# Multi-query attention sandwich: which steps' row sums go to TensorE, where the turned maxima land, and how wo is loaded

## The chip, the cores and the metric

One NeuronCore of one Trainium2 chip runs the whole program. The metric is device microseconds of one execution. An instruction sits on one of five engines: PE (TensorE), DVE (VectorE), ACT (ScalarE), POOL (GpSimd) and SP (SyncE, which here only issues DMAs).

## The reference, cut to what matters

`x` is 2 x 2048 tokens of 1024 numbers, in float32. There are 32 query heads of 32 numbers, and a single head of keys and values that all of them share.

```
def attn(x, wq, wk, wv, wo):
    q = (x @ wq).reshape(B, T, 32, 32); k = x @ wk; v = x @ wv
    scores = einsum('bqhd,bkd->bhqk', q, k) / sqrt(32), causal
    probs = softmax(scores)
    return einsum('bhqk,bkd->bqhd', probs, v).reshape(B, T, C) @ wo
x = x + layernorm(attn(layernorm(x), wq, wk, wv, wo))
x = x + layernorm(ffn(layernorm(x)))      # 8 routed low-rank experts, softmax router
```

The softmax needs, for each query and head, the maximum of its scores and the sum of the exponentials over all keys. The change touches who forms that sum.

## The kernel before, in words

**Units.** Tokens are cut into 8 blocks of 512 (4 for each of the two sequences). A block has 8 units n of 4 heads, so there are 64 units. `qb_of(n)` is the block's place in its sequence, 0 to 3. Block b has the units 8b to 8b+7, and u = n % 8. A unit goes through its keys in steps of 128 keys: `steps(n)` is 4, 8, 12 or 16. The last four steps of a unit lie on the causal diagonal, and their tiles are 512, 384, 256 and 128 queries wide. Each step has 4 slots, one for each head g; slot j is step j // 4, head j % 4. The units of blocks 3 and 7 (units 24 to 31 and 56 to 63) have 16 steps, 64 slots.

**A step.** For each slot PE forms the transposed scores of one head into one of two PSUM banks (`scores`, L1299 to L1312), and ACT takes the exponential into the SBUF ring `pr`, which holds NS = 3 steps (`exps`, L707 to L715). PE multiplies the finished step with the values (`values`, L1314 to L1327) in the next step, at g = 1, or at g = 2 for a diagonal step, whose triangle POOL first sets to zero (`mask`, L621 to L627). The sum over keys is split: for most steps POOL adds the four heads' tile into `ds` (`add`, L604 to L619). For the steps that `by_pe` names, PE multiplies the tile with a column block of ones instead and accumulates in PSUM bank PAUX (L1328 to L1336). `sum_keys` (L1352 to L1359) then adds ds's column sums in the same bank, in slot 6 of the next unit, and DVE takes reciprocals there and scales the result (L953 to L961).

**Who waits for the sums.** ACT may write step k of the ring only when step k - 3 was used by both its readers: `exps` waits for `pv_done` of step k - 3, and, if POOL sums that step, for `added`. POOL runs in the order of its loop (L647 to L663): at step t first mask(t), which waits for all four exponentials of step t, and then add(t - 1). The first add of a unit takes steps 0 and 1 together (L616), all later ones are L619.

**Maxima.** For coming units PE also forms the scores in the other orientation (`max_scores`, L1286 to L1297) into a ring of NPM = 3 PSUM banks, and DVE takes their maxima (L931 to L940). When a unit's maxima are complete, PE turns them into rows (`max_rows`, L1339 to L1350) in PAUX, ACT copies them to `mT` (L705), and four DMAs of SP (L517) put them below the stacked queries. That must be there before the unit's first scores.

**Order of the rest.** Everything else is spread over the slots of the units by `pieces` (L113 to L163): projections of queries ("q"), of keys and values ("kv"), of the output ("proj"), the router and experts, the norms of the next block. Each engine goes through its own slots in order, so a piece that waits holds up all that stands behind it on that engine. Bank PX is shared by these pieces: `BEFORE` (L446 to L465) lists who had it last, and `bank_left` waits until that one was copied out. `value_turn` (L1385 to L1392) turns the next block's values once in u = 5, in PAUX. SP's list has the loads: `wo` in one DMA of 4 MB in unit 3, "ffn" in unit 1.

## Time and profile before

| | |
|---|---|
| median of 3 runs | 3544.06 us (3539.41 to 3547.18) |
| the profiled execution | 3543.98 us, its span 3542.2 us |
| mean granted TensorE clock | 0.968 |
| PE busy | 3302.0 us, 93% of the span |
| DVE busy | 2292.4 us, 65% |
| POOL busy | 2121.0 us, 60% |
| ACT busy | 1570.5 us, 44% |

A row of the timeline gives start, duration, engine, line, operation, out<-in, how many instructions it merges, and in brackets how long the engine stood idle before it and what ended that. A row of the chain gives start, length and the line that the end of the program goes back to at that moment. A float32 product is shown as two matmul records, so x8 in a row of L1326 or L1335 is one step's four heads.

### The profile page before, as it was taken

How to read it: one execution, taken by the hardware profiler on the slowest of the kernel's cores; microseconds unless marked ns; L12 is line 12 of the kernel's file. 1: busy time of each engine (PE TensorE's matmuls, PEld its weight loads, DVE VectorE, ACT ScalarE, POOL GpSimd, SP SyncE). 2: the span in 40 equal slices, each digit the busy share in tenths (PEclk: the TensorE clock that was granted, in tenths of full speed). 3: DMA queues.
4: the chain of work that ended last, by engine and by line, in shares of the span. 5: the costliest groups of instructions: out<-in, count | busy, mean ns of one | idle time of the engine just before them, and what ended most of it. 6: DMA issues, size and time to landing. Idle time of an engine off the chain costs nothing.

```text
span 3542.2 us, 45007 instructions
## 1 busy us (share of the span) xinstructions
PE 3302.0 (93%) x15784; PEld 1611.6 (45%) x15784; DVE 2292.4 (65%) x5974; ACT 1570.5 (44%) x3124; POOL 2121.0 (60%) x773
## 2 busy tenths in 40 slices
PE   7889999999999999999888999999999999999997
PEld 3444444444544444443444444444445444444433
DVE  4666766677767677773455667766677676666605
ACT  2324444444545444455322244444445454445552
POOL 1325676666666777767322266666666677766870
PEclk9989999999999999999998899999999999999998
DMA  4412111111101010010111121111011010001000
GB/s 117 114 46 67 48 43 37 53 29 40 37 22 54 22 34 28 22 37 16 61 54 43 46 67 45 36 37 61 27 36 35 25 28 28 28 28 28 27 1 24
DMA packets 132898, 144.01 MB, mean 41 GB/s; under 512 B 28088, under 2 KB 93624, under 8 KB 132672
## 3 DMA queue, kind: packets, MB, share of 16 engines
q1 hardware_dynamic: 132368, 140.72, 13.6%
q8 instruction: 125, 2.05, 0.2%
q14 instruction: 101, 0.83, 0.1%
q10 hardware_dynamic: 304, 0.41, 0.0%
HBM read 72.91 MB, written 16.78 MB: 25 GB/s over the span
## 4 chain that ended last, share of the span: by engine, by line
PE 58%; POOL 21%; DVE 10%; issue 5%; ACT 4%; SPq 1%; DMA 1%; POOLq 0%; ACTq 0%; DVEq 0%
POOL ds L619 15%; PE ps L1308 10%; PE ps L1326 10%; PE ps L1420 9%; PE ps L1296 8%; PE ps L1282 8%; DVE mx L940 4%; POOL ds L616 3%; ACT pr L715 2%; PE ps L1335 2%; PE ps L1357 2%; PE ps L1449 2%; POOL xr L636 1%; PE ps L1461 1%; PE ps L1381 1%
## 5 line engine op out<-in xcount | busy, mean ns | idle before, releaser
L715 ACT ACTIVATE pr<-ps 128x512 f32<-128x512 f32 (+3 forms) x2560 | 1304.7, 533 | 1533.3 <-PE ps L1308 1044.8
L619 POOL TENSOR_TENSOR ds<-ds,pr 128x2048 f32<-128x2048 f32 (+1 forms) x376 | 1518.6, 4039 | 189.3 <-ACT pr L715 161.2
L1308 PE MATMUL ps<-qs,ks 98*128 98x512 f32 (+3 forms) x2560 | 1368.5, 540 | 79.8 <-ACT pr L715 66.5
L940 DVE TENSOR_REDUCE mx<-ps 128x1 f32<-128x512 f32 x1536 | 996.9, 682 | 432.1 <-PE ps L1296 427.0
L1296 PE MATMUL ps<-ks,qs 96*128 96x512 f32 (+3 forms) x2560 | 970.7, 389 | 34.5 <-DVE mx L940 19.1
L1308 PEld LDWEIGHTS ps<-qs,ks 98*128 98x128 f32 x2560 | 492.3, 193 | 767.8 <-ACT pr L715 486.2
L937 DVE CUSTOM_DVE_ANT_0 ps<-ps,mask_qk 128x128 f32<-128x128 f32 (+3 forms) x1024 | 491.8, 497 | 438.4 <-PE ps L1296 434.5
L1326 PE MATMUL ps<-pr,vs 128*32 128x512 f32 (+3 forms) x5120 | 616.3, 554 | 6.9 <-POOL pr L626 6.8
L1296 PEld LDWEIGHTS ps<-ks,qs 96*128 96x128 f32 x2560 | 497.9, 196 | 269.6 <-issue 138.6
L1282 PE MATMUL ps<-xT,wq_sb 128*128 128x512 f32 x1024 | 525.4, 613 | 14.0 <-DVE ks L1001 9.7
L616 POOL TENSOR_TENSOR ds<-pr 128x2048 f32<-128x2048 f32 (+1 forms) x64 | 273.8, 4278 | 354.8 <-ACT pr L715 354.8
L1420 PE MATMUL ps<-wo_sb,ao 128*128 128x512 f32 x896 | 459.6, 610 | 24.3 <-DVE q L929 24.3
L626 POOL TENSOR_SCALAR_AFFINE_SELECT pr<-pr 128x512 f32<-128x512 f32 x192 | 123.2, 642 | 365.4 <-ACT pr L715 365.0
L956 DVE RECIPROCAL ps<-ps 128x128 f32<-128x128 f32 x256 | 244.3, 956 | 109.8 <-PE ps L1357 109.6
L1282 PEld LDWEIGHTS ps<-xT,wq_sb 128*128 128x128 f32 x1024 | 184.4, 192 | 177.8 <-issue 158.5
L1420 PEld LDWEIGHTS ps<-wo_sb,ao 128*128 128x128 f32 x896 | 160.6, 192 | 158.9 <-issue 119.4
L1326 PEld LDWEIGHTS ps<-pr,vs 128*32 128x32 f32 x5120 | 102.0, 109 | 194.1 <-issue 160.0
L645 POOL TENSOR_TENSOR xr<-xr,zs 128x1024 f32<-128x1024 f32 x28 | 66.1, 2361 | 201.7 <-ACT zs L769 201.7
L937 DVE DVE_READ_ACCUMULATOR2_ANT mx<- 128x1 f32 x1024 | 145.4, 142 | 0.0
L929 DVE TENSOR_TENSOR q<-ps,q 128x512 fp32r<-128x512 f32 x64 | 44.3, 692 | 124.8 <-ACT q L699 124.6
L615 POOL COPY ds<-pr 128x512 f32<-128x512 f32 x16 | 9.8, 609 | 157.2 <-ACT pr L715 157.2
L1335 PE MATMUL ps<-pr,ones 128*32 128x512 f32 (+3 forms) x1088 | 102.9, 451 | 0.0
(161 smaller groups left out, 1962.5 us busy)
## 6 DMA issues: line engine op xcount, KB each, us to landing
qs<-q SPq DMA_DIRECT2D x762, 64.0 KB, 2.0
wq_sb<-in_L_attn_wq_dram SPq DMA_DIRECT2D x64, 512.0 KB, 4.3
t<-in_L_attn_x_dram SPq DMA_DIRECT2D x32, 512.0 KB, 6.4
xr<-in_L_attn_x_dram SPq DMA_DIRECT2D x28, 512.0 KB, 3.6
out_dram<-xr SPq DMA_DIRECT2D x28, 512.0 KB, 2.6
wo_sb<-in_L_attn_wo_dram SPq DMA_DIRECT2D x1, 4096.0 KB, 14.5
qs<-mT SPq DMA_DIRECT2D x252, 4.0 KB
xT<-in_L_attn_x_dram SPq DMA_DIRECT2D x4, 512.0 KB, 5.3
```

What stands on the lines that cost most here:

```text
L616: nc.gpsimd.tensor_tensor(ds[:, :, c0:], first[:, :, c0:], this, ALU.add).then_inc(added, 1)
L619: nc.gpsimd.tensor_tensor(ds[:, :, c0:], ds[:, :, c0:], this, ALU.add).then_inc(added, 1)
L715: nc.scalar.activation(pr[:, k % NS, g, c0:], ps[:, PST + head(n, t, g) % NPS, c0:], ACT.Exp, scale=SCALE).then_inc(exp_done, 1)
L937: nc.vector.tensor_tensor_reduce(out=seen, in0=seen, in1=mask_qk[:, BLK - w:], op0=ALU.add, op1=ALU.max, scale=1.0, scalar=3.0 * NEG, accu ...
L940: nc.vector.tensor_reduce(found, seen, AX.X, ALU.max).then_inc(mx_done, 1)
L956: nc.vector.reciprocal(part, part).then_inc(rden_ready, 1)
L1282: last = nc.tensor.matmul(ps[:, PX, :], wq_sb[:, n % NW, k, :], xT[:, k, :], start=(k == 0), stop=(k == KT - 1))
L1296: nc.tensor.matmul(ps[:, bank, 0:w], qs[0:STK, n % NS, g, qt * P:(qt + 1) * P], ks[0:STK, c:c + w], start=True, stop=True).then_inc(mx_rea ...
L1308: last = nc.tensor.matmul(ps[:, bank, c0:], ks[0:STK + 2, c:c + P], qs[0:STK + 2, n % NS, g, c0:], start=True, stop=not by_mask)
L1326: last = nc.tensor.matmul(ps[g * HD:(g + 1) * HD, PPV, c0:], vs[:, row, :], pr[:, (UNIT_STEP[n] + t) % NS, g, c0:], start=(t == 0), stop=( ...
L1335: last = nc.tensor.matmul(ps[g * HD:(g + 1) * HD, PAUX, c0:], ones[:, :], pr[:, (UNIT_STEP[n] + t) % NS, g, c0:], start=(t == first), stop ...
L1420: last = nc.tensor.matmul(ps[:, PX, :], ao[:, (n + k) % NAO, j % TB * P:(j % TB + 1) * P], wo_sb[:, k, h * HALF:(h + 1) * HALF], start=(k ...
```

## The change

It has five parts.

1. `by_pe(n)` now gives a tuple of steps. In units of `qb_of` 2 it is (8, 9, 10, 11), as before. In units of `qb_of` 3 it is (5, 8, 11, 14, 15) for all u, where it was steps 12 to 15 for u = 0 to 5 and steps 10 to 15 for u = 6 and 7. POOL adds the others, so steps 12 and 13 too. `adds_in` counts POOL's adds; every wait on `added` uses it.
2. The turned maxima go to the ring of the maxima: the list `RING` has all users of the three banks in PE's order, and `max_bank_left` waits for the one three places earlier, be it a maximum (DVE) or rows (ACT's copy). PAUX is so free from the reciprocals on; the first PE sum of a unit waits for `ao_ready` of the unit before.
3. `value_turn` uses bank PX and its order of users ("vt" is in `BEFORE`); it stands in slot 10 (16-slot units) or N // 2, where it stood in slot 11 or N // 2 + 1, behind the "q" pieces of that slot.
4. `wo` is loaded in eight DMAs of 512 KB, two in each of units 2 to 5; the first "proj" waits for all of them.
5. "ffn" goes from slot 8 to slot 0 of unit 1 in SP's list.

```diff
     def by_pe(n):
-        if qb_of(n) < 2:
-            return 0
-        return TB + 2 if qb_of(n) == 3 and n % NU >= 6 else TB
+        return ((), (), (8, 9, 10, 11), (5, 8, 11, 14, 15))[qb_of(n)]
+
+    def adds_in(n, t):
+        return sum(x not in by_pe(n) for x in range(1, max(t, 1) + 1))
...
-        UNIT_ADD.append(UNIT_ADD[-1] + steps(n_) - 1 - by_pe(n_))
+        UNIT_ADD.append(UNIT_ADD[-1] + adds_in(n_, steps(n_) - 1))
...
+    def rows_slot(n):
+        return slots(n - 1) // 2 + max(4, slots(n - 1) // 8)
+
+    RING, PLACE, ROWS_PLACE = [], [], []
+    for k_ in range(HEADS + 1):
+        while len(ROWS_PLACE) < UN and (goal(len(ROWS_PLACE) - 1, rows_slot(len(ROWS_PLACE))) if ROWS_PLACE else FIRST_GOAL) <= k_:
+            ROWS_PLACE.append(len(RING))
+            RING.append(("rows", len(ROWS_PLACE) - 1))
+        if k_ < HEADS:
+            PLACE.append(len(RING))
+            RING.append(("max", k_))
...
+        if n and u == 5 and blk < LAST:
+            turned = 10 if N == 16 else N // 2
+            put(turned, "PE", "vt", blk + 1)
+            put(turned, "DVE", "vt", blk + 1)
...
-            at(64 + 32, "SP", "ffn")
-            at(64 * 3 + 32, "SP", "wo")
+            at(64 + 2, "SP", "ffn")
+            for k in range(KT):
+                at(64 * (2 + k // 2) + 4 + 16 * (k % 2), "SP", "wo", k)
...
-            if u == 5 and blk < LAST:
-                turned = 11 if N == 16 else N // 2 + 5 - apart * 2
-                put(turned, "PE", "vt", blk + 1)
-                put(turned, "DVE", "vt", blk + 1)
...
         def by_gpsimd(n, t):
-            return t < steps(n) - by_pe(n)
+            return t not in by_pe(n)
...
-                            sp.dma_start(wo_sb[:, :, :], wo_v).then_inc(wo_loaded, 16)
+                            sp.dma_start(wo_sb[:, a[0], :], wo_v[:, a[0], :]).then_inc(wo_loaded, 16)
...
-                    if 2 <= t <= steps(n) - by_pe(n):
+                    if t >= 2 and by_gpsimd(n, t - 1):
                         add(n, t - 1)
-                if not by_pe(n):
+                if by_gpsimd(n, steps(n) - 1):
                     add(n, steps(n) - 1)
...
-                nc.scalar.copy(mT[:, :], ps[0:2 * GH, PAUX, :]).then_inc(mt_sb, 1)
+                nc.scalar.copy(mT[:, :], ps[0:2 * GH, PM + ROWS_PLACE[n] % NPM, :]).then_inc(mt_sb, 1)
...
+            def max_bank_left(place):
+                if place >= NPM:
+                    before, y = RING[place - NPM]
+                    pe.wait_ge(mx_done if before == "max" else mt_sb, y + 1)
...
-                if k >= NPM:
-                    pe.wait_ge(mx_done, k - NPM + 1)
-                bank, c = PM + k % NPM, key_slot(n, c) * BLK
+                max_bank_left(PLACE[k])
+                bank, c = PM + PLACE[k] % NPM, key_slot(n, c) * BLK
...
-                first = steps(n) - by_pe(n)
-                if t >= first:
-                    if t == first and n + 1 < UN:
-                        pe.wait_ge(mt_sb, n + 2)
-                    if t == first and n + 1 == UN:
+                if t in by_pe(n):
+                    if t == by_pe(n)[0]:
                         pe.wait_ge(ao_ready, n)
...
             def max_rows(n):
                 pe.wait_ge(mz_ready, 2 * (n + 1))
-                if n >= 2:
-                    pe.wait_ge(ao_ready, n - 1)
-                if n == 0:
-                    pe.wait_ge(v_sb, 1)
-                if n % NU == 6 and n + NU < UN:
-                    pe.wait_ge(v_sb, n // NU + 2)
+                max_bank_left(ROWS_PLACE[n])
...
             def sum_keys(n):
                 pe.wait_ge(added, UNIT_ADD[n + 1])
-                if n + 1 < UN:
-                    pe.wait_ge(mt_sb, n + 2)
+                if n and not by_pe(n):
+                    pe.wait_ge(ao_ready, n)
+                if n == 0:
+                    pe.wait_ge(v_sb, 1)
...
             def value_turn(blk):
                 pe.wait_ge(k_act, 2 * (blk + 1))
                 if blk:
-                    pe.wait_ge(ao_ready, NU * (blk - 1) + 5)
+                    bank_left("vt", blk)
...
-                        pe.wait_ge(wo_loaded, 16)
+                        pe.wait_ge(wo_loaded, 16 * KT)
```

## Rows read from the trace of the kernel before

**Rows 1.** The page: busy time of PE, and the chain that ended last, by engine.
```profile
PE 3302.0 (93%) x15784; PEld 1611.6 (45%) x15784; DVE 2292.4 (65%) x5974; ACT 1570.5 (44%) x3124; POOL 2121.0 (60%) x773
...
PE 58%; POOL 21%; DVE 10%; issue 5%; ACT 4%; SPq 1%; DMA 1%; POOLq 0%; ACTq 0%; DVEq 0%
```

**Rows 2.** Busy times, whole units of blocks 3 and 7: the sum of sixteen windows.
```profile
sum 1165.20, PE 1111.98 PEld 521.96 DVE 694.12 ACT 597.59 POOL 854.63; mean PE 69.50 PEld 32.62 DVE 43.38 ACT 37.35 POOL 53.41
```

**Rows 3.** Busy times, steps 5 to 13 only: units 25, 30, 61, and the sixteen's sum.
```profile
1210.70:1258.70 48.00, 47.62 (x201) 22.59 (x201) 29.72 (x76) 21.16 (x40) 44.24 (x13) 1.00 0.04 12
...
1599.80:1638.90 39.10, 35.53 (x169) 14.76 (x169) 10.52 (x40) 20.55 (x39) 31.09 (x8) 0.96 0.00 1
...
3289.10:3330.80 41.70, 35.12 (x156) 15.17 (x156) 24.01 (x63) 20.93 (x39) 40.28 (x11) 0.88 0.04 14
...
sum 717.40, PE 687.28 PEld 312.37 DVE 365.97 ACT 346.64 POOL 643.97; mean PE 42.96 PEld 19.52 DVE 22.87 ACT 21.67 POOL 40.25
```

**Rows 4.** Waits of ACT: block 3, then block 7 (total us, times, longest).
```profile
ACT pr L715 <- POOL ds L619: 47.1, 28, 2.9
ACT pr L715 <- POOL ds L616: 9.8, 7, 1.4
...
ACT pr L715 <- POOL ds L619: 51.4, 27, 4.5
```

**Rows 5.** Chain of waits through unit 30 (start, length, what).
```profile
1583.02 0.26 PE ps L1335 x8
...
1588.99 4.59 POOL ds L616
...
1628.75 0.86 PE ps L1335 x8
...
1640.57 0.65 PE ps L1335 x8
...
1643.35 0.43 PE ps L1335 x8
```

**Rows 6.** Timeline of POOL, end of unit 15 (eight steps, all added by POOL).
```profile
635.77 0.64 POOL L626 TENSOR_SCALAR_AFFINE_SELECT pr<-pr 128x512 f32<-128x512 f32 x1 [3.11 <-ACT pr L715]
...
641.48 3.45 POOL L619 TENSOR_TENSOR ds<-ds,pr 128x1536 f32<-128x1536 f32 x1
644.89 0.63 POOL L626 TENSOR_SCALAR_AFFINE_SELECT pr<-pr 128x512 f32<-128x512 f32 x1
```

**Rows 7.** Timeline of POOL, masks of steps 13 and 15 of units 25 and 30.
```profile
1258.03 0.63 POOL L626 TENSOR_SCALAR_AFFINE_SELECT pr<-pr 128x512 f32<-128x512 f32 x1
...
1266.35 0.64 POOL L626 TENSOR_SCALAR_AFFINE_SELECT pr<-pr 128x512 f32<-128x512 f32 x1 [2.26 <-ACT pr L715]
...
1639.03 0.64 POOL L626 TENSOR_SCALAR_AFFINE_SELECT pr<-pr 128x512 f32<-128x512 f32 x1 [3.20 <-ACT pr L715]
...
1644.42 0.63 POOL L626 TENSOR_SCALAR_AFFINE_SELECT pr<-pr 128x512 f32<-128x512 f32 x1 [1.76 <-ACT pr L715]
```

**Rows 8.** Timeline of PE, two passes of unit 25 one behind the other.
```profile
1240.16 0.40 PE L1308 MATMUL ps<-qs,ks 98*128 98x512 f32 x1
1240.40 0.39 PE L1296 MATMUL ps<-ks,qs 96*128 96x512 f32 x1
```

**Rows 9.** Timeline of PE and DVE, unit 53, slots 24 and 25.
```profile
2748.94 0.40 PE L1296 MATMUL ps<-ks,qs 96*128 96x512 f32 x1
2749.28 1.07 PE L1326 MATMUL ps<-pr,vs 128*32 128x512 f32 x8
...
2751.89 1.10 PE L1282 MATMUL ps<-xT,wq_sb 128*128 128x512 f32 x2 [1.55 <-DVE ks L1001]
```

**Rows 10.** Timeline behind the turned rows of unit 14.
```profile
550.63 0.69 DVE L940 TENSOR_REDUCE mx<-ps 128x1 f32<-128x512 f32 x1 [1.88 <-PE ps L1296]
```

**Rows 11.** Timeline at the boundary of units 3 and 4.
```profile
147.34 2.46 SPq L517 DMA_DIRECT2D qs<-mT  x4
...
152.05 0.80 PE L1308 MATMUL ps<-qs,ks 98*128 98x512 f32 x1 [1.94 <-DMA qs<-mT]
```

More of the change, by code:

```diff
@@ L155, in pieces @@
             put(first + apart * TB, "DVE", "scale", n - 1)
-            if u == 5 and blk < LAST:
-                turned = 11 if N == 16 else N // 2 + 5 - apart * 2
-                put(turned, "PE", "vt", blk + 1)
-                put(turned, "DVE", "vt", blk + 1)
         if n + 1 < UN:
             for who in ("PE", "ACT", "SP"):
-                put(N // 2 + max(4, N // 8), who, "rows", n + 1)
+                put(rows_slot(n + 1), who, "rows", n + 1)
         return found
@@ L460, in shared_bank @@
                             order.append((stage, 2 * a[0] + a[1]))
-                        elif stage == "wt":
-                            order.append(("wt", a[0]))
+                        elif stage in ("wt", "vt"):
+                            order.append((stage, a[0]))
             return dict(zip(order, [("", 0)] + order))
@@ L473, in adds_to @@
         def adds_to(n, t):
-            return UNIT_ADD[n] + max(t, 1)
+            return UNIT_ADD[n] + adds_in(n, t)
         def step_of(k):
@@ L617, in add @@
                 else:
-                    pool.wait_ge(added, UNIT_ADD[n] + t - 1)
+                    pool.wait_ge(added, UNIT_ADD[n] + adds_in(n, t) - 1)
                     nc.gpsimd.tensor_tensor(ds[:, :, c0:], ds[:, :, c0:], this, ALU.add).then_inc(added, 1)
@@ L933, in maximum @@
                 k = head(n, s, g)
-                seen, found = ps[:, PM + k % NPM, 0:w], mx[:, qt * GH + g, c_:c_ + 1]
+                seen, found = ps[:, PM + PLACE[k] % NPM, 0:w], mx[:, qt * GH + g, c_:c_ + 1]
                 dve.wait_ge(mx_ready, head(n, s, g) + 1)
@@ L1007, in value_turn @@
                 nc.vector.tensor_copy(vs[:, t:t + TB, :],
-                                      ps[:, PAUX, 0:TB * HD].rearrange("p (t d) -> p t d", d=HD)).then_inc(v_sb, 1)
+                                      ps[:, PX if blk else PAUX, 0:TB * HD].rearrange("p (t d) -> p t d", d=HD)).then_inc(v_sb, 1)
             def weights(i):
@@ L1273, in bank_left @@
                     pe.wait_ge(wt_done, y + 1)
+                elif before == "vt":
+                    pe.wait_ge(v_sb, y + 1)
             def project(n, k):
@@ L1335, in values @@
                         last = nc.tensor.matmul(ps[g * HD:(g + 1) * HD, PAUX, c0:], ones[:, :],
-                                                pr[:, (UNIT_STEP[n] + t) % NS, g, c0:], start=(t == first), stop=False)
+                                                pr[:, (UNIT_STEP[n] + t) % NS, g, c0:], start=(t == by_pe(n)[0]), stop=False)
                 last.then_inc(pv_done, 1)
@@ L1340, in max_rows @@
                 pe.wait_ge(mz_ready, 2 * (n + 1))
-                if n >= 2:
-                    pe.wait_ge(ao_ready, n - 1)
-                if n == 0:
-                    pe.wait_ge(v_sb, 1)
-                if n % NU == 6 and n + NU < UN:
-                    pe.wait_ge(v_sb, n // NU + 2)
+                max_bank_left(ROWS_PLACE[n])
                 for qt in range(TB):
-                    last = nc.tensor.transpose(ps[0:2 * GH, PAUX, qt * P:(qt + 1) * P],
+                    last = nc.tensor.transpose(ps[0:2 * GH, PM + ROWS_PLACE[n] % NPM, qt * P:(qt + 1) * P],
                                                mz[:, qt, :, :].rearrange("p g c -> p (g c)"), ident[:, :])
@@ L1387, in value_turn @@
                 if blk:
-                    pe.wait_ge(ao_ready, NU * (blk - 1) + 5)
+                    bank_left("vt", blk)
                 for k in range(TB):
-                    last = nc.tensor.transpose(ps[:, PAUX, k * HD:(k + 1) * HD], kv_of(blk)[3 * HD:4 * HD, k * P:(k + 1) * P],
+                    last = nc.tensor.transpose(ps[:, PX if blk else PAUX, k * HD:(k + 1) * HD], kv_of(blk)[3 * HD:4 * HD, k * P:(k + 1) * P],
                                                ident[3 * HD:4 * HD, 3 * HD:4 * HD])
```

## The prediction

> **What bounds the kernel now.** I read the page first: TensorE is busy for 93% of the span, GpSimd for 60%, and the chain that ended last lies on PE for 58% and on POOL for 21% [rows 1]. So the kernel is PE's, with stretches in which POOL sets the pace. The change acts on the sixteen units of sixteen steps (blocks 3 and 7), so I asked for busy times there: 1165.2 us, in which PE matmuls are busy 1112.0 [rows 2]. All that POOL costs them is inside the missing 53.2 us. In steps 5 to 13 alone, where the relief is meant to come, PE is idle for 717.4 - 687.3 = 30.1 us [rows 3]. It is uneven: 0.4 us in unit 25 (u = 1 to 3 are full of projections), 3.6 in unit 30, 6.6 in unit 61. ACT waits for POOL's later adds longer than PE stands idle, 47.1 + 51.4 = 98.5 us [rows 4], because PE works on two banks ahead and has other pieces. The difference is cover, not gain.
>
> **The PE sums.** One step's sum costs PE 0.86, 0.65, 0.43 or 0.26 us at 512, 384, 256 or 128 queries [rows 5]. The old steps 12 to 15 cost 2.20 us; the new 5, 8, 11, 14, 15 cost 3 x 0.86 + 0.43 + 0.26 = 3.27; u = 6 and 7 had 2.20 + 2 x 0.86 = 3.92. In total PE gets 12 x 1.07 - 4 x 0.65 = 10.2 us more work. I count it by place, because the end of the unit gets a bound of its own (below). Ahead of step 13 twelve units gain three sums, 31.0 us, and four gain one (5 and 8 come, 10 goes, 11 stays), 3.4. In about four units (u = 0, 6, 7) step 5 falls where POOL's first four adds still set the pace: step 7 can't start before them, and the chain in unit 30 stands on POOL there from 1588.99 on [rows 5]. There 0.86 is free, -3.4. Term: +31.0 us. Whether PE really has no room I take from two passes one behind the other: starts 0.24 us apart for 512 columns, no gap [rows 8].
>
> **The relief.** POOL does a full add in 4.6 us [rows 5]. With 5, 8 and 11 gone it has two adds per three steps, and these steps last over 4 us each, so its waits behind step 7 vanish. They are at least the 30.1 us of idle [rows 3] and at most the 98.5 of ACT's waits [rows 4]. A restart behind a wait hides some more under the modelled end of the matmul before it, and unit 61 also ran at a clock of 0.88 [rows 3]. I take -36, near the low end, since PE's own idleness is the nearer measure.
>
> **The end of the unit.** This is what the diff doesn't say. Steps 12 and 13 become POOL's, and its order is mask(13), add(12), mask(14), add(13), mask(15). ACT's step 15 waits for add(12), the next unit's step 0 for add(13), and PE's values(15) for mask(15). None of it can start before step 13's exponentials. The units of eight steps show just this tail now: in unit 15 from its second mask (635.77) to its last (644.89) 9.12 us pass, of them 3.45 for the 384-wide add [rows 6]. In units 24 to 27 and 56 to 59 the same stretch, mask(13) to mask(15), lasts 8.3 to 8.4 us today (8.32 in unit 25), in units 30 and 31 5.39 [rows 7]; the other six lie between in the same view, at 5.9 to 7.8. Step 12's sum no longer stands ahead of mask(13), which comes 0.86 us earlier. So a unit loses 9.12 - 0.86 - 8.32 = -0.06 us (nothing) or 9.12 - 0.86 - 5.39 = +2.9; over the sixteen it comes to 16. In unit 29 mask(13) is itself late behind add(11) by about 1.1, and PE has a few tenths ready at some ends. Bounds: 0, if PE has other work ready there, and 16. I take +14, since nothing else stands in PE's order there: `scores` needs the banks that ACT empties.
>
> **The values' turn.** In the five blocks with 32 or more slots it moves from behind the "q" pieces of slot N / 2 + 1 to slot N / 2, and it now waits for PX, that is for all three copies of keys by DVE. Today PE does slot N / 2 + 1's scores, maximum and values while DVE copies, and then still waits 1.55 us [rows 9]. With the turn in front PE stands still from the end of slot N / 2's maximum, and the covered work, 2749.28 to 2750.3 and two passes, comes behind: +1.5 us in four units. Counted the same way in the same view it is some 2.4 in unit 29, where slot 34 is cover as well, and 0.45 in the two units with 16 slots. DVE's order behind it is unhurt, since its turned copy follows the same three. Sum 9.3, bounds 0 and 9.3 (nothing if POOL set the pace right behind); I take +8.
>
> **The ring.** Rows now use one of three banks for one ACT copy. PE waits for the maximum three places back. At the time of the rows DVE has nearly always emptied the ring: behind unit 14's rows it stands idle for 1.88 us waiting for PE [rows 10]. Gain: none, as the old waits on PAUX were long met. Cost: between 0 and one maximum (0.69 us [rows 10]) for each of 64 rows, 44 us; the nearest row says the low end, I take +0.6.
>
> **The loads.** "ffn" changes its slot, but SP has nothing between slots 0 and 8 of unit 1, so its order of DMAs stays: 0. The eight wo pieces cost SP issues while it waits for rows anyway. The gain is at the end of unit 3: the row DMAs are issued by 147.34 + 2.46 = 149.8 and PE starts at 152.05 after 1.94 us of idleness [rows 11]. Part of this is the rows' own landing, so the gain is 0 to 1.9; I take -1.
>
> **Sum.** 31 - 36 + 14 + 8 + 0.6 - 1 = +16.6 us on the profiled execution's own 3543.98 us (span 3542.2), which is the median 3544.06 within 0.1. So 3560.6, say 3560 us. A measurement of this kernel can tell about 0.2%, 7 us, from no change.
>
> **Rivals.** *Faster, because PE has room.* If the sums go into gaps of PE, the +31 falls away: -36 + 14 + 8 + 0.6 - 1 = -14 us, 3530. It decides where the sums at 5, 8 and 11 stand in steps 6, 9 and 12: these must not get 0.86 us longer. For it speaks that PE was 53 us idle in these units [rows 2]; against it, that unit 25 has 0.4 of 48 us to give [rows 3] and that passes follow each other without a gap [rows 8]. The Trainium skill, Perfetto Trace Analysis, Identifying the Most-Contended Engine, says that matmul busy time is no good measure and that the busy share of weight loads should be used. Weight loads are busy for 45% [rows 1], and by that rule the sum would be the 3530 of this rival; the starts 0.24 us apart speak for the matmul row here. Chance 0.27.
>
> *No difference.* Relief of 50 instead of 36 (half of ACT's waits), or a tail that costs 5 and not 14, brings the sum to +2.6 or +7.6: 3544 to 3551, 3547 in the middle. Chance 0.20.
>
> *Slower, and more than forecast, by the clock.* Eight units (28 to 31, 60 to 63) get 2 to 4 us of PE idleness at their ends. Units 30 and 61 now, with idleness of that kind inside, ran at 0.96 and 0.88 in steps 5 to 13 [rows 3]. Were each of the eight followed by 3.4 us at half clock, that is 8 x 1.7 = 14 us more: 3574. Against it: the idleness inside these units, which pulls the clock now, goes away. Chance 0.13.
>
> *The change doesn't do what it says:* the tail binds at the end and POOL stays the pace. That is the forecast's third term; the range has it.
>
> **How the numbers follow.** Forecast (3560, its own range 3551 to 3572) 0.40, clock case 0.13, no difference 0.20, faster 0.27. Slower by over 0.2%: 0.40 x 0.92 + 0.13 = 0.50. Within 0.2%: 0.20 and the forecast's low edge, less the upper part of that rival, 0.20. Faster: 0.30, with some of the low side of the unknown terms. Low end: the faster rival with relief 46 in place of 36, -24, is 3520. High end: relief 30, turn 9.3, tail 16, ring 2, no gain by wo, is 31 - 30 + 16 + 9.3 + 2 = +28, and half of the clock case, +7, gives 3579, taken as 3580. Outside lie 2 in 10.
>
> **What would show it.** Right: no 4.7 us spacing of L619 behind step 7; the stretch mask(13) to mask(15) at 9.1 us in all sixteen units; steps 14 and 15 at 5.4 and 4.0 us in units 30, 31, 62 and 63; units 25 to 27 longer by about 2 us; ACT's waits for L619 gone in the middle and new at the end; PE idle before the turn (L1390) by some 3 us instead of before L1282; L1335 busy for about 10 us more. Wrong: units 25 to 27 no longer than now (then PE had room), the end stretch under 9 us, or a matmul clock that differs from 0.968 by more than 0.005.

## The result and the profile after

| | before | after |
|---|---|---|
| median | 3543.78 us (3539.41 to 3547.18) | 3572.9 us (3569.39 to 3578.24) |
| ratio | | 1.0086 [1.0073, 1.0099] |
| span of the profiled execution | 3542.2 us | 3573.3 us |
| mean granted TensorE clock | 0.968 | 0.965 |

The change makes the kernel 29 us slower. The page after, its busy row and its chain, against [rows 1]; then the page's group for the sums that PE does (L1335 of before is L1356 now; other lines of this part moved by 17 to 24 as well: the scores L1308 are L1332, the maxima L1296 are L1320, the values L1326 are L1350, POOL's add L619 is L636, its mask L626 is L643, ACT's exponentials L715 are L732):

```profile
PE 3318.5 (93%) x15848; PEld 1618.4 (45%) x15848; DVE 2295.1 (64%) x5974; ACT 1572.4 (44%) x3124; POOL 2069.4 (58%) x765
...
PE 68%; POOL 12%; DVE 10%; ACT 5%; issue 4%; SPq 1%; DMA 1%; ACTq 0%; POOLq 0%; DVEq 0%
...
L1356 PE MATMUL ps<-pr,ones 128*32 128x512 f32 (+3 forms) x1152 | 115.5, 474 | 0.0
```

The same group in the kernel before:

```profile
L1335 PE MATMUL ps<-pr,ones 128*32 128x512 f32 (+3 forms) x1088 | 102.9, 451 | 0.0
```

POOL gave up 51.6 us of work and its share of the chain fell from 21% to 12%, PE's rose from 58% to 68%. That is what the change was made to do, and still the span grew by 31.1 us. Where it grew is read from busy times in windows, the same stretches as in [rows 2, 3]. The sums over the sixteen units of blocks 3 and 7 of the changed kernel: the whole units, steps 5 to 13, steps 14 and 15. (PE does the sum of a step in the step behind it, so steps 5 to 13 of the kernel before hold the sum of step 12, 16 x 0.86 = 13.8 us, and its steps 14 and 15 that of step 13.)

```profile
sum 1180.70, PE 1123.44 PEld 527.11 DVE 697.23 ACT 599.42 POOL 801.95; mean PE 70.22 PEld 32.94 DVE 43.58 ACT 37.46 POOL 50.12
...
sum 703.50, PE 694.30 PEld 316.71 DVE 363.68 ACT 348.67 POOL 463.81; mean PE 43.39 PEld 19.79 DVE 22.73 ACT 21.79 POOL 28.99
...
sum 145.50, PE 121.49 PEld 63.13 DVE 94.64 ACT 44.71 POOL 144.34; mean PE 7.59 PEld 3.95 DVE 5.92 ACT 2.79 POOL 9.02
```

And of the kernel before, steps 14 and 15 (its other two sums are [rows 2, 3]):

```profile
sum 115.00, PE 110.80 PEld 56.86 DVE 76.16 ACT 44.05 POOL 18.49; mean PE 6.92 PEld 3.55 DVE 4.76 ACT 2.75 POOL 1.16
```

Steps 5 to 13 became 13.9 us shorter (717.4 to 703.5; PE's idleness in them fell from 30.1 to 9.2), steps 14 and 15 became 30.5 us longer, and POOL is busy for 144.3 of their 145.5 us, where it was busy for 18.5 of 115.0. The sixteen units together lose 15.5 us. Of these 10.2 are PE's added sums; PE's idleness grew from 53.2 to 57.3 us, 4.0; and the remaining 1.2 are, by this estimate, the same matmuls at a lower clock. The other half of the 31 us lies outside them: unit 32, right behind block 3, +2.0; of the units with the values' turn 13 +4.7, 21 +4.6, 37 +1.8 and 53 +3.0; the first eight units together +5.5; while units 38 and 39 win 7.9. The +5.5 can't be put down to the change: six kernels, the changed one and five of the experiments, differ only in who sums what from unit 24 on, and their first eight units take from 214 to 225 us (218 in the kernel before). Unit 13 scatters among them in the same way, from 51.4 to 56.0.

The end of a unit, read as in [rows 7] from the timeline of POOL, here unit 30 of the changed kernel:

```profile
1660.97 0.64 POOL L643 TENSOR_SCALAR_AFFINE_SELECT pr<-pr 128x512 f32<-128x512 f32 x1 [2.36 <-ACT pr L732]
1661.58 4.51 POOL L636 TENSOR_TENSOR ds<-ds,pr 128x2048 f32<-128x2048 f32 x1
1666.05 0.63 POOL L643 TENSOR_SCALAR_AFFINE_SELECT pr<-pr 128x512 f32<-128x512 f32 x1
1666.65 3.44 POOL L636 TENSOR_TENSOR ds<-ds,pr 128x1536 f32<-128x1536 f32 x1
1670.04 0.63 POOL L643 TENSOR_SCALAR_AFFINE_SELECT pr<-pr 128x512 f32<-128x512 f32 x1
```

That is the order that the prediction wrote down, mask(13), add(12), mask(14), add(13), mask(15): 9.07 us from the first to the last, 5.39 before [rows 7]. And the timeline of PE over the same time:

```profile
1663.30 0.33 PE L1332 MATMUL ps<-qs,ks 98*128 98x128 f32 x1 [0.29 <-ACT pr L732]
1666.50 0.47 PE L1332 MATMUL ps<-qs,ks 98*128 98x128 f32 x1 [2.87 <-ACT pr L732]
1666.90 1.08 PE L1350 MATMUL ps<-pr,vs 128*32 128x256 f32 x8
1667.76 1.08 PE L1356 MATMUL ps<-pr,ones 128*32 128x256 f32 x8
```

PE stands for 2.87 us until add(12) has ended and ACT has run once more. The row behind it is the part that wants a second look: the values and the sums of 256 queries take 1.08 us each and the score of 128 columns 0.47. In the same timeline of the kernel before they took:

```profile
1642.71 0.64 PE L1326 MATMUL ps<-pr,vs 128*32 128x256 f32 x8 [0.21 <-POOL pr L626]
1643.16 0.61 PE L1335 MATMUL ps<-pr,ones 128*32 128x256 f32 x8
1643.71 0.33 PE L1308 MATMUL ps<-qs,ks 98*128 98x128 f32 x1
```

PE came back at a lower granted clock. The busy times in windows say so; column PEclk (the third from the end) of the windows 1655 to 1665 and 1665 to 1678.6 us:

```profile
1655.00:1665.00 10.00, 7.39 (x47) 2.95 (x38) 1.48 (x6) 4.50 (x11) 4.66 (x3) 0.98 0.00 0
1665.00:1678.60 13.60, 11.71 (x59) 4.59 (x59) 1.12 (x4) 5.66 (x12) 5.67 (x4) 0.51 0.25 62
```

Full clock while PE worked, then 13.6 us at a granted clock of 0.51 (1.2 GHz is 0.5 of 2.4) that begin in the wait. Below, such a stretch is called a half-clock stretch.

The turn shows the same pair. Timeline of PE in unit 53 of the changed kernel, slot 24, for [rows 9], and the two windows around it:

```profile
2773.32 0.40 PE L1320 MATMUL ps<-ks,qs 96*128 96x512 f32 x1
2776.75 0.40 PE L1408 MATMUL ps<-ident,q 32*128 32x32 f32 x4 [3.03 <-DVE ks L1018]
2777.08 0.54 PE L1332 MATMUL ps<-qs,ks 98*128 98x512 f32 x1
```

```profile
2767.00:2777.00 10.00, 6.97 (x29) 3.21 (x28) 7.70 (x24) 5.74 (x10) 5.29 (x3) 1.00 0.00 0
2777.00:2780.40 3.40, 3.40 (x14) 1.04 (x13) 0.98 (x2) 0.60 (x1) 3.40 (x2) 0.56 0.25 105
```

Over all seven turns the waits are, in the view of waits (total us, times, longest; in the kernel before it was 9.7, 7, 1.6 in front of L1282):

```profile
PE ps L1408 <- DVE ks L1018: 19.1, 7, 3.1
```

### The profile page after: what moved, and what is told of

Same layout as the page of the kernel before. It is cut to its first block, busy times and chain, and to the rows that moved or that the text cites. A ratio compares the mean times of both kernels' runs of the same rounds, so it can differ in the third digit from the quotient of the medians.

```text
span 3573.3 us, 45096 instructions
## 1 busy us (share of the span) xinstructions
PE 3318.5 (93%) x15848; PEld 1618.4 (45%) x15848; DVE 2295.1 (64%) x5974; ACT 1572.4 (44%) x3124; POOL 2069.4 (58%) x765
## 4 chain that ended last, share of the span: by engine, by line
PE 68%; POOL 12%; DVE 10%; ACT 5%; issue 4%; SPq 1%; DMA 1%; ACTq 0%; POOLq 0%; DVEq 0%
PE ps L1332 13%; PE ps L1350 12%; PE ps L1438 11%; PE ps L1320 10%; PE ps L1301 10%; POOL ds L636 7%; DVE mx L957 4%; ACT pr L732 3%; POOL ds L633 2%; PE ps L1356 2%; PE ps L1375 2%; PE ps L1399 2%; PE ps L1467 2%; PE ps L1479 2%; DVE ps L973 1%
## 5 line engine op out<-in xcount | busy, mean ns | idle before, releaser
L732 ACT ACTIVATE pr<-ps 128x512 f32<-128x512 f32 (+3 forms) x2560 | 1305.9, 533 | 1562.4 <-PE ps L1332 1123.5
L636 POOL TENSOR_TENSOR ds<-ds,pr 128x2048 f32<-128x2048 f32 (+2 forms) x368 | 1467.6, 3988 | 263.0 <-ACT pr L732 242.5
L1332 PE MATMUL ps<-qs,ks 98*128 98x512 f32 (+3 forms) x2560 | 1373.2, 542 | 82.5 <-ACT pr L732 69.0
L1320 PE MATMUL ps<-ks,qs 96*128 96x512 f32 (+3 forms) x2560 | 970.3, 389 | 33.9 <-DVE mx L957 18.6
L1332 PEld LDWEIGHTS ps<-qs,ks 98*128 98x128 f32 x2560 | 493.3, 193 | 775.5 <-ACT pr L732 480.2
L1350 PE MATMUL ps<-pr,vs 128*32 128x512 f32 (+3 forms) x5120 | 620.4, 558 | 7.3 <-POOL pr L643 7.1
L1320 PEld LDWEIGHTS ps<-ks,qs 96*128 96x128 f32 x2560 | 499.5, 197 | 268.0 <-issue 140.7
L643 POOL TENSOR_SCALAR_AFFINE_SELECT pr<-pr 128x512 f32<-128x512 f32 x192 | 123.6, 644 | 362.6 <-ACT pr L732 362.3
L1350 PEld LDWEIGHTS ps<-pr,vs 128*32 128x32 f32 x5120 | 102.1, 109 | 196.0 <-issue 158.9
L1356 PE MATMUL ps<-pr,ones 128*32 128x512 f32 (+3 forms) x1152 | 115.5, 474 | 0.0
```

Of the source, the lines that this page charges most:

```text
L636: nc.gpsimd.tensor_tensor(ds[:, :, c0:], ds[:, :, c0:], this, ALU.add).then_inc(added, 1)
L732: nc.scalar.activation(pr[:, k % NS, g, c0:], ps[:, PST + head(n, t, g) % NPS, c0:], ACT.Exp, scale=SCALE).then_inc(exp_done, 1)
L1320: nc.tensor.matmul(ps[:, bank, 0:w], qs[0:STK, n % NS, g, qt * P:(qt + 1) * P], ks[0:STK, c:c + w], start=True, stop=True).then_inc(mx_rea ...
L1332: last = nc.tensor.matmul(ps[:, bank, c0:], ks[0:STK + 2, c:c + P], qs[0:STK + 2, n % NS, g, c0:], start=True, stop=not by_mask)
L1350: last = nc.tensor.matmul(ps[g * HD:(g + 1) * HD, PPV, c0:], vs[:, row, :], pr[:, (UNIT_STEP[n] + t) % NS, g, c0:], start=(t == 0), stop=( ...
L1356: last = nc.tensor.matmul(ps[g * HD:(g + 1) * HD, PAUX, c0:], ones[:, :], pr[:, (UNIT_STEP[n] + t) % NS, g, c0:], start=(t == by_pe(n)[0]) ...
```

## The experiments

All medians stand against the kernel before, run on the same chip beside them (3542.2 to 3544.4 us). What a unit takes is the time from its first exponentials to the next unit's. Differences between two kernels are differences of their ratios times 3544, with the intervals' half widths added as squares; they are good to 4 to 8 us, while the length of one undisturbed unit (without a half-clock stretch that comes and goes) repeats from kernel to kernel within 0.1 us. So the medians say whether, and the units say where. In several places below the growth of a group of units is split in three: the PE sums that were added or taken away, at the prices of [rows 5]; PE's idleness, the length less the busy time; and the rest of the busy time, which is the same matmuls at another clock. The split is an estimate from the busy times of one trace each.

### The old choice of sums, all else changed

```diff
-        return ((), (), (8, 9, 10, 11), (5, 8, 11, 14, 15))[qb_of(n)]
+        return ((), (), (8, 9, 10, 11), (10, 11, 12, 13, 14, 15) if n % NU >= 6 else (12, 13, 14, 15))[qb_of(n)]
```

> The changed kernel, but by_pe names the old steps (12 to 15, and 10 to 15 for u = 6 and 7); ring, turn and loads stay changed. Theory A (the values' turn costs more than the sums, since the TensorE clock falls where PE stands still ahead of it): the sixteen-step units give back some 10 us, so 3563 us, 19 above the kernel before. Rival B (the sums and the ends of the units are most of the loss, the turn only its 8 us): 3552 us.

Measured: 3551.68 us, 1.0019 [1.0010, 1.0028]. So the choice of sums costs 1.0086 - 1.0019, 24 +- 6 us, and turn, ring and loads together 7. Of the two sizes offered the rival's is the right one: the sums' part is larger than the forecast's 9 us (31 - 36 + 14).

### The tail: 12 and 13 to POOL, and in the middle only step 11 taken from it (u = 0 to 5)

```diff
-        return ((), (), (8, 9, 10, 11), (5, 8, 11, 14, 15))[qb_of(n)]
+        return ((), (), (8, 9, 10, 11), (10, 11, 14, 15) if n % NU >= 6 else (11, 14, 15))[qb_of(n)]
```

> e1_old_steps with steps 12 and 13 given to POOL: PE sums steps 11, 14, 15 (10, 11, 14, 15 for u = 6 and 7). Theory A (the end of the unit: step 15 waits for add 12, the next unit for add 13): the stretch mask(13) to mask(15) is 9.1 us in all sixteen units, units 30, 31, 60 to 63 lose 2 to 4 us each, some 20 us over e1_old_steps: 3571 us. Rival C (the ends are covered and the loss sits in the sums at 5, 8 and 11): PE has 8 us less work, 3545 us.

Measured: 3584.73 us, 1.0120 [1.0103, 1.0136], 14 us above what was expected. The tail costs what was expected of it and more, although PE here has one or two sums fewer per unit than with the old choice: 36 +- 7 us by the medians, and by the units 20.7 in the sixteen and 3.3 in unit 32. Units 30, 31 and 32 run at a mean clock of 0.90, 0.91 and 0.84; with the old choice all three had 1.00.

### The middle alone: 5, 8 and 11 to PE, which keeps 12 and 13

```diff
-        return ((), (), (8, 9, 10, 11), (5, 8, 11, 14, 15))[qb_of(n)]
+        return ((), (), (8, 9, 10, 11), (5, 8, 11, 12, 13, 14, 15))[qb_of(n)]
```

> e1_old_steps with the sums at 5, 8 and 11 added on PE and 12 to 15 kept there: PE sums 5, 8, 11, 12, 13, 14, 15. Theory A: +31 us of PE work, -36 us of waits for POOL, 3547 us; no lengthening of the ends. Rival C: PE's work is paid in full and the relief is half of what was taken, 3570 us.

Measured: 3547.72 us, 1.0008 [0.9995, 1.0021], as expected, and 4 us under the kernel with the old choice (6 us either way, so no different from it by the median alone; its sixteen units are 3.6 us shorter). Busy times of its sixteen units: whole, steps 5 to 13, steps 14 and 15.

```profile
sum 1163.80, PE 1131.79 PEld 530.25 DVE 694.33 ACT 599.69 POOL 674.22; mean PE 70.74 PEld 33.14 DVE 43.40 ACT 37.48 POOL 42.14
...
sum 715.80, PE 706.66 PEld 320.06 DVE 364.91 ACT 348.69 POOL 463.21; mean PE 44.17 PEld 20.00 DVE 22.81 ACT 21.79 POOL 28.95
...
sum 115.10, PE 111.32 PEld 57.33 DVE 77.20 ACT 44.20 POOL 18.36; mean PE 6.96 PEld 3.58 DVE 4.82 ACT 2.76 POOL 1.15
```

This kernel is the cleanest witness. PE is busy for 19.8 us more than in [rows 2], POOL for 180 less, and the sixteen units end 1.4 us earlier. Two engines traded work and the time hardly moved. And the difference between this kernel and the change is nothing but the place of sums 12 and 13: 1180.7 - 1163.8 = 16.9 us in the sixteen units and 2.3 in unit 32 behind them, 19.2 us, by the medians 28 +- 7. (The units see 19. This kernel's own runs reach from 3538.75 to 3560.35, and the profiled one, 3557.87, is 10 above their median, while the change's, 3575.01, is 2 above its own; the two profiled spans differ by 17.2. Units 15, 22 and 54 of this trace, for instance, have half-clock stretches that the change's trace has not, and are 1.6 to 3.6 us longer.)

By unit, the change minus this kernel: -0.2, 0, -0.8, -0.8, -0.1 in units 24 to 28, -0.3, 0.2, -0.1, 0, 1.9 in units 56 to 60, together nothing; 3.4, 2.9, 5.7, 2.5, 1.4, 1.1 in units 29, 30, 31, 61, 62, 63, together 17.0, and 2.3 in unit 32. Split in three, the 16.9 us of the sixteen units are -24.2 for PE's two missing sums, +25.3 of idleness (32.0 to 57.3) and +15.8 by the clock; unit 32, where PE is busy for 30.0 instead of 26.8 us, adds 3 to the last. So the tail takes 24 us of work from PE, and PE pays with 25 in standing idle and some 19 in the clock.

### Step 13 given back to PE, and step 12 given back

```diff
-        return ((), (), (8, 9, 10, 11), (5, 8, 11, 14, 15))[qb_of(n)]
+        return ((), (), (8, 9, 10, 11), (5, 8, 11, 13, 14, 15))[qb_of(n)]
```

> The changed kernel, but in the units of query block 3 PE takes step 13 back, so that POOL sums 6, 7, 9, 10 and 12 of them. Theory A (what costs is the order at the end of the unit: PE's in-order sums of 14 and 15 wait for POOL's last sum before them, and each such wait may bring a stretch at granted clock 0.5): POOL's last sum ahead of 14 is now 12, step 13's sum needs no POOL row, so about half of the 25 us between the middle-only kernel (3547.7) and the change (3572.9) goes: 3559, from 3554 to 3565. Rival B (what costs is the number of sums that each engine has, whichever they are): PE has one sum more per unit, 16 x 0.86 = 14 us of it, POOL one less: 3573 to 3587.

The other one has (5, 8, 11, 12, 14, 15).

> The changed kernel, but in the units of query block 3 PE takes step 12 back, so that POOL sums 6, 7, 9, 10 and 13 of them. Theory A (order at the end of the unit): POOL still has step 13 right ahead of PE's 14, but reaches it one sum earlier, with no queue of two sums behind step 11: 3557, from 3552 to 3565, and mask 13 to mask 15 between 7 and 9 us. Rival B (number of sums): 3573 to 3587. If the loss belongs to 13 alone (the last sum before PE's own), this run stays near 3572 and the kernel that gives POOL step 12 falls to near 3548.

Measured: with 12 on POOL 3560.35 us, 1.0046 [1.0032, 1.0061]; with 13 on POOL 3568.37, 1.0071 [1.0054, 1.0088]. The number of sums is out as the cause: PE has 10 us more work in the first (0.65 a unit, [rows 5]) and 14 in the second (0.86), and neither is slower than the change. The first lies where the theory of order put it; the second is 3 us above its upper end and 5 under the rival's lower one, and its stretch from mask 13 to mask 15, expected at 7 to 9 us, is 9.4 in u = 1 to 3 and 6.4 in units 30 and 31. By units 24 to 32 and 56 to 63, each keeps most of the loss: against the middle-only kernel both are some 16 us longer, the change 19. By the medians they are 13 +- 7 and 22 +- 8 longer, the change 28 +- 7. So by the units one late sum on POOL is nearly as bad as two, whichever it is; the medians leave open that giving back 13 wins half. Timeline of PE at the end of unit 30, step 12 on POOL:

```profile
1653.98 0.33 PE L1332 MATMUL ps<-qs,ks 98*128 98x128 f32 x1 [2.24 <-ACT pr L732]
1654.23 0.64 PE L1350 MATMUL ps<-pr,vs 128*32 128x256 f32 x8
1654.69 0.61 PE L1356 MATMUL ps<-pr,ones 128*32 128x256 f32 x8
...
1657.43 0.66 PE L1350 MATMUL ps<-pr,vs 128*32 128x128 f32 x8
1657.86 0.65 PE L1356 MATMUL ps<-pr,ones 128*32 128x128 f32 x8
```

The wait is 2.24 us in place of 2.87, and the half-clock stretch follows it all the same, only later: the sum of 256 queries still takes 0.61 us, as before the change, but that of 128 takes 0.65 where the kernel before has 0.40.

### Work that adds zero, put into the wait

Products of a zero weight with `wo_sb`, accumulated into a PSUM bank, which leave what is there as it is: eight in slot 61 (the last step) of units 29 to 31 and 61 to 63, and eight in the second slot of the unit behind each. A group of eight takes PE 1.9 us, all eleven 21.2. (The diff leaves out the tile `zero` and its setting to zero by POOL.)

```diff
+                    late = lambda m: m >= 0 and qb_of(m) == 3 and m % NU >= 5
+                    if (j == 61 and late(n)) or (j == 1 and late(n - 1)):
+                        for x in range(2):
+                            for g_ in range(GH):
+                                nc.tensor.matmul(ps[g_ * HD:(g_ + 1) * HD, PAUX, :], zero[:, :], wo_sb[:, x, 0:BLK],
+                                                 start=False, stop=False)
```

> The changed kernel with products of a zero weight added to PE's stream: in the units with query block 3 of the last three K/V blocks (u of 5 or more) two groups of four behind the scores of the last step but two, two groups in the second step of the next unit, which add zero to a PSUM bank and change nothing of the result. Theory A (part of the loss at the end of the unit comes through the clock, PE standing idle there brings the stretches at granted clock 0.5 which begin at 1603, 1665 and 1730 us of the changed kernel): those stretches vanish or shorten, and although PE has some 20 us of products more, most of it in time in which it stood, the whole is 3558 to 3573. Rival B (the wait costs by itself, the clock falls of its own accord): the stretches stay, and 3573 to 3585.

Measured: 3565.08 us, 1.0064 [1.0047, 1.0080], as expected by theory A and 8 +- 7 us less than the change, with 21 us more of products on PE. Its timeline at the end of unit 30, for the one of the changed kernel above (L1334 are the scores, L1352 the values, L1358 the sums, L1516 the zero products):

```profile
1661.00 0.33 PE L1334 MATMUL ps<-qs,ks 98*128 98x128 f32 x1 [0.29 <-ACT pr L734]
1661.25 1.92 PE L1516 MATMUL ps<-wo_sb,zero 128*32 128x512 f32 x16
1664.22 0.33 PE L1334 MATMUL ps<-qs,ks 98*128 98x128 f32 x1 [1.04 <-ACT pr L734]
1664.48 0.64 PE L1352 MATMUL ps<-pr,vs 128*32 128x256 f32 x8
1664.94 0.61 PE L1358 MATMUL ps<-pr,ones 128*32 128x256 f32 x8
```

Idle for 1.04 us where it was 2.87, the sum of 256 queries takes 0.61, and none of the half-clock rows follows (the next such stretch begins 17 us behind the last row, at 1683). Busy times of unit 32, first of the changed kernel, then of this one:

```profile
1735.30:1765.50 30.20, 30.02 (x134) 14.09 (x133) 16.14 (x54) 9.05 (x21) 8.08 (x5) 0.87 0.37 119
```

```profile
1731.50:1758.80 27.30, 27.12 (x142) 12.64 (x134) 14.79 (x50) 8.77 (x21) 8.17 (x5) 1.00 0.40 128
```

Unit 32 has eight of the added products and is 2.9 us shorter. The stretches of the changed kernel behind the ends of units 29, 30 and 31 (they begin at 1603, 1665 and 1730) are gone, all three. So the clock's fall there is caused by the idleness. Over units 28 to 32 the filler gains 4 us net (320.3 us in the change, 316.2 here): PE has six groups, 11.5 us, more to do, but is busy for only 2.5 more (295.9 to 298.4), so the better clock takes 9 us off, and its idleness falls by 6.6. Against the middle-only kernel (306.0) the change loses 14.3 us in these five units: -6.0 for the missing sums, +8.5 of idleness and +11.8 by the clock. So there the clock is the larger part of the tail's price. In units 61 to 63 the filler gains nothing (198.6 against 197.7); the change has only two stretches of 3.4 us in units 60 and 61.

### The turn alone, the turn a slot later, the turn undone

Alone: the kernel before, with this and the waits that go with the bank PX.

```diff
+        if n and u == 5 and blk < LAST:
+            turned = 10 if N == 16 else N // 2
+            put(turned, "PE", "vt", blk + 1)
+            put(turned, "DVE", "vt", blk + 1)
...
-                    pe.wait_ge(ao_ready, NU * (blk - 1) + 5)
+                    bank_left("vt", blk)
```

> The kernel before with the values' turn alone changed (bank PX, slot 10 or N // 2). Theory A: some 22 us above before, 3566 us, with the granted clock at half for 3.4 or 6.8 us just at the turn of five units. Rival B: 8 us, 3552 us.

Measured: 3553.00 us, 1.0025 [1.0013, 1.0036], 9 us: the rival's number, though the half-clock stretches of theory A are there. PE's wait at the turn grew by 1.4 us a unit (9.7 to 19.2 over seven), and five of the seven units are longer by more than that: 13 by 3.1, 21 by 4.6, 29 by 5.3, 37 by 1.8, 53 by 3.0 (unit 45 is as long as before, and unit 5 lies in the stretch that scatters). Units 38 and 39 behind unit 37 are 7.8 shorter, since half-clock stretches that they had (mean clock 0.83 and 0.79) moved away (1.00 and 0.94). So the net of 9 hides 18 in these five units against 8. (The first eight are 7 longer here, which is within what they scatter by.)

One slot later, in the changed kernel:

```diff
-            turned = 10 if N == 16 else N // 2
+            turned = 11 if N == 16 else N // 2 + 1
```

> The changed kernel with the values' turn one slot later (slot 11 or N // 2 + 1), still ahead of the q pieces, so that one slot's scores, maximum and values stand ahead of its wait. Theory A: PE's wait ahead of the turn falls from 3.1 to about 1.6 us, the clock no longer falls there, and units 13, 21, 29, 45 and 53 win 3 to 4 us each: 3557 us. Rival B: only the cover comes back, 5 times 1 us: 3568 us.

Measured: 3566.12 us, 1.0067 [1.0052, 1.0082], 7 +- 7 less than the change, nearer to the rival. The wait is 1.55 to 1.64 us, and behind it the clock still falls in units 13, 29, 37 and 45, not in 21 and 53. Units 13, 21, 29 and 53 fall by 2.9, 4.2, 3.2 and 2.6, but unit 39 takes back 4.0 and 38 1.3: its stretches return (0.94, 0.79).

Undone: the change with the turn at its old place behind the "q" pieces and in PAUX. PAUX can't hold the turn and a sum of step 5 at once, so in units with u = 5 that sum is POOL's.

```diff
-        return ((), (), (8, 9, 10, 11), (5, 8, 11, 14, 15))[qb_of(n)]
+        return ((), (), (8, 9, 10, 11), (8, 11, 14, 15) if n % NU == 5 else (5, 8, 11, 14, 15))[qb_of(n)]
```

> The changed kernel with the values' turn back in bank PAUX behind the q pieces (slot 11 or N // 2 + 1), and in u = 5 of block 3 and 7 the steps 8, 11, 14, 15 on PE, as the turn needs PAUX until step 8. Theory A: units 13, 21, 29, 45 and 53 win 3 to 5 us each, units 38 and 39 lose 8 as their half-clock stretch comes back: 3563 us. Rival B: 3568 us or more.

Measured: 3570.23 us, 1.0071 [1.0053, 1.0089], no different from the change (5 +- 8 us less), the rival's number. Unit 29 falls by 6.7, 13, 21, 45 and 53 by 1.6 to 4.6; 38 and 39 take back 7.7, and units 61 and 62 are 7.6 longer. So the turn is worth 9 us on the kernel before and nothing that a median can tell on the changed one. This run can't price it alone, though: unit 61 has no turn, and what it and unit 62 lose is more likely the price of step 5's sum on POOL, which no run tells apart.

### The loads alone

```diff
-            at(64 + 32, "SP", "ffn")
-            at(64 * 3 + 32, "SP", "wo")
+            at(64 + 2, "SP", "ffn")
+            for k in range(KT):
+                at(64 * (2 + k // 2) + 4 + 16 * (k % 2), "SP", "wo", k)
```

> The kernel before with the loads alone changed (wo in eight pieces, ffn in slot 0 of unit 1). Theory A: the order of SP's list around ffn is the same and the pieces take idle time of the queue: 3543 us within 3 us, PE's wait for the row DMAs at the start of unit 4 shorter by up to 1.9 us. Rival B: the first eight units, 5.5 us longer in the changed kernel, are so by the loads: 3549 us.

Measured: 3543.73 us, 1.0000 [0.9991, 1.0009]. Nothing. With the old choice of sums the ring comes on top of turn and loads, and that kernel (3551.68) is not above the turn alone (3553.00): the ring is nothing, too (-2 +- 5 us).

### A choice of sums that pays

If the tail must stay PE's, and POOL needs relief where it sets the pace, one sum in the middle should do. Turn as before, ring and loads as changed, and:

```diff
-        return ((), (), (8, 9, 10, 11), (5, 8, 11, 14, 15))[qb_of(n)]
+        if qb_of(n) < 3:
+            return ((), (), (8, 9, 10, 11))[qb_of(n)]
+        u = n % NU
+        if u == 0:
+            return (5, 12, 13, 14, 15)
+        if u < 5:
+            return (8, 12, 13, 14, 15)
+        if u == 5:
+            return (8, 12, 13, 14, 15) if n // NU < LAST else (8, 11, 12, 13, 14, 15)
+        return (5, 10, 12, 13, 14, 15)
```

> A version meant to beat both: turn as in the kernel before, rows in the ring, loads in pieces, and PE's steps chosen by what each unit needs: 12 to 15 always, so that the ends stay short, and 5 (u = 0), 8 (u = 1 to 5), 5 and 10 (u = 6 and 7), 8 and 11 (unit 61), where POOL sets the pace. By theory A the middles win 2 to 3 us in units 24, 30, 31, 56, 62 and 63, 0.5 to 1 us in u = 1 to 5, 6 us in unit 61, and nothing is lost: 3522 us. Rival C (PE's work is paid in full): 14 us more of it, 3550 us.

Measured: 3528.62 us, 0.9954 [0.9940, 0.9969], faster than both kernels, and 7 us above the 3522 that was expected. Of its sixteen units (whole, steps 5 to 13, steps 14 and 15):

```profile
sum 1151.70, PE 1115.30 PEld 525.00 DVE 695.02 ACT 599.91 POOL 796.19; mean PE 69.71 PEld 32.81 DVE 43.44 ACT 37.49 POOL 49.76
...
sum 703.00, PE 690.45 PEld 316.00 DVE 369.49 ACT 349.55 POOL 584.50; mean PE 43.15 PEld 19.75 DVE 23.09 ACT 21.85 POOL 36.53
...
sum 114.90, PE 109.98 PEld 55.92 DVE 73.90 ACT 43.49 POOL 18.16; mean PE 6.87 PEld 3.50 DVE 4.62 ACT 2.72 POOL 1.14
```

Its steps 5 to 13 are as short as the change's (703.0 against 703.5) with one or two sums of PE's ahead of step 12 where the change has three, and with step 12's own sum in them, which the change has not; its steps 14 and 15 are those of before.

Steps 5, 8 and 11 all three, with the tail kept, in units 30, 31, 61 and 62 (the text before the run names some others; the edit is in these four); against the kernel just shown:

```diff
-        u = n % NU
+        u, last = n % NU, n // NU == LAST
...
-            return (8, 12, 13, 14, 15) if n // NU < LAST else (8, 11, 12, 13, 14, 15)
-        return (5, 10, 12, 13, 14, 15)
+            return (5, 8, 11, 12, 13, 14, 15) if last else (8, 12, 13, 14, 15)
+        return (5, 10, 12, 13, 14, 15) if last and u == 7 else (5, 8, 11, 12, 13, 14, 15)
```

> The kernel before with the loads in eight pieces and the maxima's ring, and another choice of the sums that PE does: the last four of every 16-step unit and step 8, or 5, as in the kernel that ran in 3528.6; here the units of block 6 and unit 31 have step 11 too. Theory A (where POOL is late in the middle of a unit, PE's relief of it is worth more than the 0.86 us that it costs): the units 28 to 31 and 60, 61 fall by 1 to 3 us each, 3519, from 3515 to 3525. Rival B (the choice of the kernel at 3528.6 has all there is to get, one more sum costs its 0.86 us each): 3529 to 3533.

Measured: 3525.65 us, 0.9948 [0.9933, 0.9963], just above the upper edge of what was expected, and not to be told from the one before. Units 30 and 31 fall by 0.5 and 0.8 where 1 to 3 was expected; only unit 61 falls much, from 69.7 to 63.2 us, its clock from 0.93 to 1.00. Its sixteen units take 1144.1 us, 21 less than in [rows 2].

## Why the prediction was right in direction and short in size

Forecast 3560 with 3520 to 3580, measured 3572.9. Term by term, with the runs that weigh it:

| term | forecast | measured | by |
|---|---|---|---|
| sums and relief, steps 5 to 13 | +31 - 36 = -5 | -3.6 in the units, -4 +- 6 in the medians | middle alone against the old choice |
| end of the unit | +14 | +19 in the units, 28 +- 7 in the medians | the change against middle alone |
| turn | +8 | +9 +- 4 | turn alone |
| ring | +0.6 | -2 +- 5 | old choice against turn alone |
| loads | -1 | 0 +- 3 | loads alone |

**The sums have no room on PE.** This was the step on which direction hung, and it held: step 6 of unit 25 went from 5.4 to 6.3 us and step 9 from 4.8 to 5.7, 0.9 each, as a sum of 0.86 says. L1356 is busy for 12.6 us more, forecast 10. The rival "faster, because PE has room" is refuted by these steps and by the middle-only kernel, where 19.8 us more on PE and 180 less on POOL gave 1.4. The chain had said so too: what POOL left of it, PE took.

**The relief** is where it was looked for: step 7 of units 30 and 31 fell from 4.7 to 2.7 and 2.4 us; ACT's waits for POOL's later adds in blocks 3 and 7 fell from 98.5 us [rows 4] to 46.8, and to 7.8 in the middle-only kernel, so most of what is left stands at the new ends. PE's idleness in steps 5 to 13 fell by 21 of the 30.1 us, and the clock there rose (unit 30 from 0.96, unit 31 from 0.91 and unit 61 from 0.88, all to 1.00), as the prediction argued against its clock case. The -36 is not confirmed by itself, only the sum with the +31.

**The end of the unit is the term that was mis-sized**, and only in part. By place the step was right: the prediction priced the tail at -0.06 us in the units full of projections and +2.9 in those like 30. Against the middle-only kernel the ten units up to u = 4 lose nothing, though their stretch from mask 13 to mask 15 grew as well (to 9.56 us in u = 1 to 4 rather than the 9.12 taken from unit 15), and the six with u of 5 or more lose 17.0. The rule of the prediction, 9.12 - 0.86 less the old stretch (its own 1.1 for unit 29), gives 8.4 us for units 60 to 63, which lost 6.9, but 6.8 for units 29 to 31, which lost 12.0, and unit 32 behind them 2.3 more. The excess sits where the half-clock stretches are. What the term left out is the clock: the prediction put it into a rival at 0.13, eight units times 1.7 us. Unit 31's mean clock is 0.89 and unit 32's 0.87, both 1.00 in the middle-only kernel; the filler shows that the idleness causes it, and that undoing it there gives back 9 us of PE's time, 4 net of the filler. Against the middle-only kernel the clock's part is about 19 us (15.8 and 3). Against the kernel before, which has such stretches inside these units, it is only 1.2 in the sixteen and 3.3 in unit 32, so the rival's 14 us, meant against that kernel, was three times too much: the old stretches went as the new ones came. That its 3574 lies next to the measured 3572.9 is luck. What the medians show beyond the units, 28 against 19, is in part that the one trace of the middle-only kernel is of a slower run than its median; the rest stays open.

**The turn's** size was right by luck of cancellation. The wait did grow as worked out: 19.1 us over seven turns against 9.7, 3.03 in unit 53, where 1.5 + 1.55 were added up. But a half-clock stretch of 3.4 or 6.8 us begins at each of the seven turns of the changed kernel (granted clock 0.56 in the window shown), so with the turn alone units 13, 21, 29 and 53 lose 3 to 5 us in place of 1.5 (2.4 in unit 29); and a stretch moved there is missing later, in units 38 and 39, which win 8. Neither was in the sum.

**What the prediction named as signs:** most came true. The end stretch is 9.1 to 9.6 us in all sixteen units; steps 14 and 15 last 5.4 and 4.0 us in units 30 and 62 and 5.4 and 4.1 in unit 31, but 4.7 and 2.9 in unit 63, the last one; units 25 to 27 are longer, but by 2.0, 0.7 and 0.7 where 2 was said of all three. ACT's waits for L636 (L619 of before) did move to the ends, and PE's to the turn. The mean clock moved by 0.003, inside the 0.005 at which the forecast would have been called wrong, and still the clock had a part in it: a mean over 3573 us is too coarse for stretches of 3.4 to 13.7 us.

The Trainium skill (Perfetto Trace Analysis, Identifying the Most-Contended Engine) judges how near TensorE is to its roof by the share of peak FLOPs and by the weight loads' busy share, here 45%, and not by the matmuls', here 93%. Read as the forecast's rival read it, as room for more sums, this would have given 3530. This case's traces speak against that reading: in unit 25 the added sums of steps 5 and 8, 0.86 us each, made steps 6 and 9 longer by 0.9 us each.

## What to carry to other kernels

When work is shared between a fast engine and a slow helper, it isn't the amount that decides but where in the order the helper's last piece stands: give it pieces early and never those just ahead of a point at which the fast engine has nothing else, since one late piece of 4.5 or 3.4 us cost 16 us in the units where two cost 19. Price a hand-over at each place by the row of a unit that already ends that way, and treat an idle stretch of 2 to 3 us on TensorE as dearer than it looks: read the granted clock of the windows right behind it, not the mean over the kernel. And where a helper is behind by a little, take one piece from it, not three.

## What the runs showed of the hardware

Waits of 2.24, 2.87 and 3.03 us of PE were each followed by a half-clock stretch (granted clock 0.51 and 0.56 in the windows shown), in which a score of 128 columns goes from 0.33 to 0.47 us and a sum of 256 queries from 0.61 to 1.08. With a wait of 1.04 us in the place of the 2.87, made so by 1.9 us of products with a zero weight, there was none. The wait's length alone doesn't decide it: behind the wait of 3.01 us at the turn of unit 13 the middle-only kernel has no such stretch for 19 us, and waits of 1.5 us in units 30 and 31 were followed by one in the kernel before and by none with the old choice of sums in the changed kernel. In all, 21 us of useless work made the program no longer, and by the median shorter. And such stretches are not local: those of units 38 and 39 went and came back with the place of the turn in unit 37 (the two units together take 55.7 to 55.9 us in the eight kernels with the turn in the new place, 63.4 to 63.7 in the five with it in the old one), 8 us in units that the edit didn't touch.
